# The two experts' weights by a tanh in the last stage of a graph and expert kernel

## The chip, the cores and the metric

The kernel runs on one core of a Trainium2 chip. The metric is the time of one execution on the device, in microseconds (us). A few runs of one kernel are given by their median.

## The reference

The input is x, 12,500 nodes of 256 features, with 212,500 weighted edges. A graph layer comes first (two rounds of a weighted sum over edges, with products by W1 and W2 and a batch norm between), and its result is added to x. Then comes a layer of 8 experts with the two best for each node:

```python
    x = x + _L0_gnn_ref(_layernorm(x, axis=-1), src, dst, edge_weight, L0_gnn_W1, L0_gnn_W2, L0_gnn_gamma, L0_gnn_beta)
    x = x + _L0_ffn_ref(_layernorm(x, axis=-1)[None], ...)[0]
...
            logits = tokens.astype(jnp.float32) @ router_w.astype(jnp.float32).T
            probs = jax.nn.softmax(logits, axis=-1)
            rw, re = jax.lax.top_k(probs, TOP_K)
            if TOP_K > 1:
                rw = rw / jnp.maximum(rw.sum(-1, keepdims=True), 1e-12)
            combine = jnp.zeros((N, E), tokens.dtype).at[jnp.arange(N)[:, None], re].set(rw)
            out = tokens
            for e in range(E):
                h = jax.nn.gelu(tokens @ w1[e] + b1[e], approximate=False)
                y = h @ w2[e] + b2[e]
                out = out + combine[:, e:e + 1] * y
```

With a and b the two largest logits of a node, the two weights are exp(a)/(exp(a)+exp(b)) and its complement to 1. That is 0.5 + 0.5 tanh((a-b)/2) and 0.5 - 0.5 tanh((a-b)/2).

## The kernel before

The program is written out by hand, engine by engine, with semaphores. The last stage (`pe_last`, `act_last`, `dve_last`, `pool_last`, `sp_last`) does three things at once. It gathers the rows of h2 for the second round of the graph layer, it makes the norm and the router's gates of a superblock, and it runs the 8 experts of the superblock before.

The nodes lie in 100 blocks of R = 125. SBS cuts them into 27 superblocks: 23 of 4 blocks and then 4 of 2 blocks. `moe_order` is called with the same order on every engine. In round t it takes three streams: the gather's chunks of superblock t, `first` (norm and router) of superblock t-1, and the experts of superblock t-2 (`up` is the first product with its Gelu, `down` the second product). After each expert's `up` it resumes `first` for one part, up to its next `yield`. Each `tick()` within them does one gather chunk.

A gather chunk is 128 gathered rows G (GpSimd, L1537). Two chunks of three are split: ScalarE writes the high half gH = G times weight (L1605), VectorE the low half gL (L1584), and TensorE multiplies both by a one-hot matrix (L1626, L1628). The third chunk stays whole (ScalarE L1601, TensorE L1624). VectorE makes the one-hot matrices, four chunks at once (L1571; L1567 for a block's tail). ScalarE and VectorE prepare a chunk LEAD = 5 chunks ahead of its product.

An expert's `up` is L1733 on TensorE, the Gelu at L1833 and the high half at L1838 on ScalarE, the low half at L1982 on VectorE; `down` is L1754 on TensorE and L1998 on VectorE, which adds the weighted result to Z. Both have two PSUM banks in turn.

The router is a part of `first`. TensorE multiplies by the router's weights (L1699) and signals d2_lg. VectorE takes the largest logit (L1929), subtracts it (L1931) and signals rt_s; then comes a tick. ScalarE waits for rt_s, takes Exp in place (L1812) and signals rt_e; it then does three ticks. VectorE waits for rt_e, sums (L1934), inverts (L1936) and multiplies (L1938). It then finds the eight largest in order, one MAX8 a block (L1941), and their positions, with one MATCH_VALUE_LOAD and one FIND_INDEX8 a block (L1944); a tick follows. Then it converts the positions (L1947), adds the two largest (L1948), bounds, inverts and multiplies (L1950, L1952, L1954), puts each of the two weights in its expert's place (L1958, L1959, one each a block), and adds the two (L1961), which signals rt_c; the third tick follows. TensorE waits for rt_c to turn the gates C (L1708), which ScalarE copies (L1820) for the product with b2 (L1714).

Earlier in `first` the norm takes its root on ScalarE (L1790, Sqrt), between VectorE's variance (L1895) and its reciprocal (L1898). ScalarE's loads of activation tables (ACT_TABLE_LOAD) are put in by the compiler and carry the line of the activation behind them. Every wait is on the waiting engine's own queue, in program order.

Of the kernel before, what the change touches and what calls it, by code (L numbers as in the profile page):

```python
# [9 lines left out]
ALU = mybir.AluOpType  # L10
ACT = mybir.ActivationFunctionType
AX = mybir.AxisListType
# [5 lines left out]
R = 125  # L18
# [137 lines left out]
def pairs_before(i):  # L156

    return sum(n // 2 for b, n in SBS[:i])


def l2_before(i, ex):

    return NEXP * pairs_before(i) + ex * (SBS[i][1] // 2)
# [31 lines left out]
def build(nc, x, src, dst, ew, W1, W2, gamma, beta, rw, w1, b1, w2, b2, out, force=None):  # L195
# [13 lines left out]
    with ExitStack() as ctx:  # L209
        def sb(name, shape, dt=F32):  # L210
            return ctx.enter_context(nc.sbuf_tensor(name, shape, dt))

        def sem(name):
            return ctx.enter_context(nc.semaphore(name))

        ident = sb("ident", [P, P])
        iota_f = sb("iota_f", [P, P])
# [189 lines left out]
        d2_tt, d2_tc, tsp, d2_lg, d2_k, rt_s, rt_e, rt_c = (sem(n) for n in ("d2_tt", "d2_tc", "tsp", "d2_lg", "d2_k", "rt_s", "rt_e", "rt_c"))  # L407
# [1101 lines left out]
        def bank(i, name, k=0):  # L1509

            z = SBS[i][1] // 2
            return psum[6 + ({"tr": 0, "z": 2, "tt": 2 + z, "lg": 4 + z, "ct": 5 + z, "b2": 6 + z}[name] + k) % 2]
# [249 lines left out]
        def act_last(e, B, gathered):  # L1762
            if gathered:
                for c in range(LEAD):
                    act_prepare(e, B, c)

            def chunks(t):
                b0, n = SBS[t]
                for o in range(b0 * KC, (b0 + n) * KC) if gathered else ():
                    if o + LEAD < NB * KC:  # L1770
                        act_prepare(e, B, o + LEAD)
                    yield

            def first(i, tick):
                b0, n = SBS[i]
                v, rt, TT = small[0:R, 570:598], B.rt, B.tT
                if i == 0:
                    e.wait_ge(wsp, 4 * WP)
                for k in range(2):
                    e.wait_ge(d2_tr, 2 * i + k + 1)  # L1780
                    if i and k == 0:
                        e.wait_ge(d2_z, pairs_before(i))
                    e.activation(B.zT[:, k * 512:k * 512 + n * R], bank(i, "tr", k)[:, 0:n * R], ACT.Copy).then_inc(d2_cp, 1)
                tick()
                yield
                for h in range(0, n, 2):
                    tick()
                yield
                e.wait_ge(d2_v, i + 1)
                e.activation(v[:, 12:12 + n], v[:, 8:8 + n], ACT.Sqrt).then_inc(d2_sq, 1)  # L1790
                tick()
                tick()
                yield
                for k in range(2):
                    e.wait_ge(d2_tt, 2 * i + k + 1)
                    if i and k == 0:
                        e.wait_ge(d2_lg, i)
                    if i >= 2 and k == 0:
                        e.wait_ge(l1s, 16 * (i - 1))
                    c_ = slice(k * 512, k * 512 + n * R)  # L1800
                    e.activation(TT[:, c_], bank(i, "tt", k)[:, 0:n * R], ACT.Copy).then_inc(d2_tc, 1)
                    e.activation(B.tH[i % 2][:, c_], bank(i, "tt", k)[:, 0:n * R], ACT.Copy).then_inc(d2_tc, 1)
                e.wait_ge(d2_k, 2 * (i + 1))
                for j in range(n):
                    c_ = slice(j * F, (j + 1) * F)
                    m = e.activation(B.Z(i)[:, c_], B.xt[:, c_], ACT.Identity, bias=v[:, 24 + j:25 + j], scale=v[:, 20 + j:21 + j])
                m.then_inc(d2_o, 1)
                tick()
                yield
                p8 = rt[:, 8:8 + 8 * n]  # L1810
                e.wait_ge(rt_s, i + 1)
                e.activation(p8, p8, ACT.Exp).then_inc(rt_e, 1)  # L1812
                tick()
                tick()
                tick()
                yield
                e.wait_ge(d2_ct, i + 1)
                if i:
                    e.wait_ge(d2_b2, pairs_before(i))
                e.activation(B.cT[:, 0:n * R], bank(i, "ct")[0:8, 0:n * R], ACT.Copy).then_inc(d2_cc, 1)  # L1820
                yield
                for h in range(0, n, 2):
                    tick()

            def up(i, ex, tick):
                n = SBS[i][1]
                for m_ in range(2):
                    q = 2 * (NEXP * i + ex) + m_
                    tick()
                    tick()  # L1830
                    f = psum[2 + q % 2][:, 0:n * R]
                    e.wait_ge(l1s, q + 1)
                    e.activation(f, f, ACT.Gelu, bias=b1T[:, ex, m_:m_ + 1]).then_inc(gel, 1)  # L1833
                    e.wait_ge(gel, q + 1)
                    if q >= 4:
                        o = NEXP * i + ex - 1
                        e.wait_ge(l2s, l2_before(o // NEXP, o % NEXP))
                    e.activation(B.hH[ex % 2][:, m_ * 512:m_ * 512 + n * R], f, ACT.Copy).then_inc(hhi, 1)  # L1838

            def down(i, ex, tick):  # L1840
                for j in range(SBS[i][1]):
                    tick()
            moe_order(chunks, first, up, down, nothing)

        def dve_last(e, B, own, gathered):
# [29 lines left out]
            def first(i, tick):  # L1875
                b0, n = SBS[i]
                Zs, X, C, rt = B.Z(i), B.xt, B.comb[i % 2], B.rt
# [41 lines left out]
                L = bank(i, "lg")[0:R, 0:8 * n].rearrange("p (b e) -> p b e", e=8)  # L1919

                def r(at, w=1):
                    return rt[:, at:at + n * w] if w == 1 else rt[:, at:at + n * w].rearrange("p (b e) -> p b e", e=w)

                def wide(a):
                    return a.rearrange("p (b o) -> p b o", o=1).broadcast_to([R, n, 8])
                p8, m8 = r(8, 8), r(48, 8)
                ix, ixf = rt[:, 88:88 + 8 * n].bitcast(U32), r(128, 8)
                e.wait_ge(d2_lg, i + 1)
                own.done(e.tensor_reduce(r(0), L, AX.X, ALU.max))  # L1929
                e.wait_ge(own.s, own.n)  # L1930
                e.tensor_tensor(p8, L, wide(r(0)), ALU.subtract).then_inc(rt_s, 1)  # L1931
                tick()
                e.wait_ge(rt_e, i + 1)
                own.done(e.tensor_reduce(r(0), p8, AX.X, ALU.add))  # L1934
                e.wait_ge(own.s, own.n)
                own.done(e.reciprocal(r(4), r(0)))  # L1936
                e.wait_ge(own.s, own.n)
                own.done(e.tensor_tensor(p8, p8, wide(r(4)), ALU.mult))  # L1938
                e.wait_ge(own.s, own.n)
                for j in range(n):  # L1940
                    own.done(e.max(m8[:, j, :], p8[:, j, :]))  # L1941
                e.wait_ge(own.s, own.n)
                for j in range(n):
                    own.done(e.max_index(ix[:, 8 * j:8 * j + 8], m8[:, j, :], p8[:, j, :]))  # L1944
                tick()
                e.wait_ge(own.s, own.n)
                own.done(e.tensor_copy(rt[:, 128:128 + 8 * n], ix))  # L1947
                own.done(e.tensor_tensor(r(0), m8[:, :, 0], m8[:, :, 1], ALU.add))  # L1948
                e.wait_ge(own.s, own.n)
                own.done(e.tensor_scalar(r(0), r(0), 1e-12, None, ALU.max))  # L1950
                e.wait_ge(own.s, own.n)
                own.done(e.reciprocal(r(4), r(0)))  # L1952
                e.wait_ge(own.s, own.n)
                own.done(e.tensor_tensor(m8, m8, wide(r(4)), ALU.mult))  # L1954
                e.wait_ge(own.s, own.n)
                g0, g1 = r(168, 8), r(208, 8)
                for j in range(n):
                    own.done(e.tensor_scalar(g0[:, j, :], iota_f[0:R, 0:8], ixf[:, j, 0:1], m8[:, j, 0:1], ALU.is_equal, ALU.mult))  # L1958
                    own.done(e.tensor_scalar(g1[:, j, :], iota_f[0:R, 0:8], ixf[:, j, 1:2], m8[:, j, 1:2], ALU.is_equal, ALU.mult))  # L1959
                e.wait_ge(own.s, own.n)  # L1960
                e.tensor_tensor(C[:, 0:8 * n].rearrange("p (b e) -> p b e", e=8), g0, g1, ALU.add).then_inc(rt_c, 1)  # L1961
                tick()
# [21 lines left out]
            def down(i, ex, tick):  # L1984
# [6 lines left out]
                for h in range(0, n, 2):  # L1991
# [4 lines left out]
                    for j in range(h, h + 2):  # L1996
                        a = Zs[:, j * F:(j + 1) * F]
                        e.scalar_tensor_tensor(a, psum[4 + q % 2][0:R, (j - h) * F:(j - h + 1) * F], C[:, 8 * j + ex:8 * j + ex + 1], a,  # L1998
                                               ALU.mult, ALU.add).then_inc(moe, 1)
            moe_order(chunks, first, up, down, nothing)  # L2000


# [503 lines left out]
```

## Time and profile before

| | |
|---|---|
| median of 3 runs | 4628.79 us (4623.98 to 4629.16) |
| the profiled execution | 4638.37 us, its span 4636.6 us |
| mean granted clock of TensorE over the span | 0.937 |
| busy over the span: TensorE | 3811.2 us, 82% |
| VectorE | 3319.8 us, 72% |
| ScalarE | 3034.7 us, 65% |
| GpSimd | 2864.8 us, 62% |
| router passes (L1929 to L1961) | 27, the first at 2159.55 us, the last at 4595.43 us |

The views name the engines PE (TensorE's products), PEld (its weight loads), DVE (VectorE), ACT (ScalarE), POOL (GpSimd) and SP (SyncE). A line such as L1929 is line 1929 of the kernel. The time in square brackets in a timeline is how long the engine stood idle before the row, with the instruction that ended the wait by the profile; "issue" and "remote" are waits for which it found none on the core. Tile names in the views are those of memory that is shared: "X" stands also for the router's tile rt and for Z.

### The profile page before, as it was taken

How to read it: one execution, taken by the hardware profiler on the slowest of the kernel's cores; microseconds unless marked ns; L12 is line 12 of the kernel's file. 1: busy time of each engine (PE TensorE's matmuls, PEld its weight loads, DVE VectorE, ACT ScalarE, POOL GpSimd, SP SyncE). 2: the span in 40 equal slices, each digit the busy share in tenths (PEclk: the TensorE clock that was granted, in tenths of full speed). 3: DMA queues.
4: the chain of work that ended last, by engine and by line, in shares of the span. 5: the costliest groups of instructions: out<-in, count | busy, mean ns of one | idle time of the engine just before them, and what ended most of it. 6: DMA issues, size and time to landing. Idle time of an engine off the chain costs nothing.

```text
span 4636.6 us, 84123 instructions
## 1 busy us (share of the span) xinstructions
PE 3811.2 (82%) x26914; PEld 3306.3 (71%) x26914; DVE 3319.8 (72%) x8731; ACT 3034.7 (65%) x6515; POOL 2864.8 (62%) x2961
## 2 busy tenths in 40 slices
PE   1688888888789999955788888888888888888988
PEld 1677877887677777744577777777777777777867
DVE  8788888888688888855466666666666666666655
ACT  3688888888777777753455555655556555555555
POOL 0377776777566666546766666666666666666541
PEclk9999999999899999975799999999999999989989
DMA  8788888887799898863333333333333333333221
GB/s 237 278 313 312 315 310 309 309 311 282 264 316 309 310 311 299 297 188 111 93 99 100 110 101 96 107 100 103 105 102 105 101 100 109 101 98 106 82 75 29
DMA packets 308793, 857.93 MB, mean 185 GB/s; under 512 B 47937, under 2 KB 133018, under 8 KB 305852
## 3 DMA queue, kind: packets, MB, share of 16 engines
q0 software_dynamic: 140032, 442.58, 29.1%
q1 hardware_dynamic: 166148, 396.53, 26.7%
q10 hardware_dynamic: 2172, 13.35, 0.8%
q8 instruction: 226, 3.70, 0.3%
q14 instruction: 215, 1.76, 0.1%
HBM read 545.71 MB, written 306.56 MB: 184 GB/s over the span
## 4 chain that ended last, share of the span: by engine, by line
PE 51%; DVE 15%; ACT 12%; issue 11%; another core or an unknown queue 6%; DMA 4%; POOL 2%; SPq 0%; ACTq 0%; DVEq 0%; POOLq 0%
PE ps L1733 10%; PE ps L1754 8%; PE ps L1624 4%; PE ps L1461 4%; PE ps L891 3%; DMA L<-msgd 3%; PE ps L849 2%; PE ps L1628 2%; PE ps L892 2%; PE ps L860 2%; PE ps L1626 2%; DVE S L1407 2%; PE ps L848 2%; ACT gH L1605 2%
## 5 line engine op out<-in xcount | busy, mean ns | idle before, releaser
L1537 POOL DMA_INDIRECT G<-h,tabT x1440 | 1481.6, 1029 | 809.5 <-issue 385.1
L956 ACT ACTIVATE A<-ps,A 128x256 f32<-128x256 f32 x1728 | 692.0, 514 | 94.0 <-PE ps L892 89.5
L1007 POOL DMA_INDIRECT msgd<-A,tabT x432 | 549.6, 1272 | 291.5 <-ACT A L956 196.5
L1833 ACT ACTIVATE ps<-ps,b1T 128x500 f32<-128x500 f32 (+1 forms) x432 | 267.7, 620 | 697.2 <-remote 381.4
L1605 ACT ACTIVATE gH<-G,tabT 128x256 fp32r<-128x256 f32 x960 | 454.4, 503 | 275.2 <-PE ps L1628 102.6
L1584 DVE SCALAR_TENSOR_TENSOR gL<-G,tabT,gH 128x256 fp32r<-128x256 f32 x960 | 448.9, 481 | 115.8 <-ACT gH L1605 59.8
L1998 DVE SCALAR_TENSOR_TENSOR X<-ps,X 125x256 f32<-125x256 f32 x800 | 347.4, 478 | 248.7 <-remote 200.6
L891 PE MATMUL ps<-winH,DT 128*128 128x256 f32 x1728 | 469.1, 304 | 63.5 <-issue 39.5
L1626 PE MATMUL ps<-gH,s 128*125 128x256 f32 x1067 | 353.0, 332 | 110.2 <-ACT gH L1605 60.1
L892 PE MATMUL ps<-winL,DT 128*128 128x256 f32 x1728 | 433.1, 283 | 0.0
L1628 PE MATMUL ps<-gL,s 128*125 128x256 f32 x1067 | 339.0, 319 | 73.9 <-DVE gL L1584 37.8
L891 PEld LDWEIGHTS ps<-winH,DT 128*128 128x128 f32 x1728 | 329.6, 191 | 80.4 <-issue 67.8
L1624 PE MATMUL ps<-G,s 128*125 128x256 f32 x960 | 329.4, 426 | 62.7 <-issue 32.4
L1626 PEld LDWEIGHTS ps<-gH,s 128*125 128x125 f32 x1067 | 217.8, 204 | 173.9 <-issue 143.1
L892 PEld LDWEIGHTS ps<-winL,DT 128*128 128x128 f32 x1728 | 331.4, 192 | 0.0
L1386 POOL TENSOR_TENSOR low<-L,mH 128x256 fp32r<-128x256 f32 x267 | 227.9, 854 | 163.3 <-issue 115.8
L946 ACT ACTIVATE DT<-ps,tabT 128x512 fp32r<-128x512 f32 x432 | 319.8, 741 | 6.3 <-DMA h<-A 4.1
L1628 PEld LDWEIGHTS ps<-gL,s 128*125 128x125 f32 x1067 | 216.9, 203 | 129.8 <-issue 57.6
L1407 DVE TENSOR_SCALAR S<-gap,L 128x125 fp32r<-128x125 f32 x1068 | 290.1, 335 | 26.8 <-DMA L<-msgd 26.7
L1388 POOL COPY tabT<-L 128x12 f32<-128x12 f32 x400 | 224.8, 576 | 131.0 <-DVE S L1407 68.4
L1352 ACT ACTIVATE mH<-L 128x1024 fp32r<-128x1024 f32 x267 | 269.2, 1046 | 49.0 <-DMA L<-msgd 48.9
L1571 DVE TENSOR_TENSOR s<-iota_f,tabT 128x500 fp32r<-128x500 f32 x400 | 268.9, 672 | 9.6 <-PE ps L1624 5.2
(338 smaller groups left out, 11076.3 us busy)
## 6 DMA issues: line engine op xcount, KB each, us to landing
L<-msgd SPq DMA_DIRECT2D x400, 520.0 KB, 5.7
A<-sbd SPq DMA_DIRECT2D x54, 861.0 KB
msgd<-A SPq DMA_DIRECT2D x100, 325.0 KB
G<-h,tabT POOLq DMA_INDIRECT x1440
winR<-h SPq DMA_DIRECT2D x108, 128.0 KB
A<-in_x SPq DMA_DIRECT2D x10, 1120.0 KB
h<-A ACTq DMA_DIRECT2D x10, 1120.0 KB
acc<-h SPq DMA_DIRECT2D x10, 1120.0 KB
```

What stands on the lines that cost most here:

```text
L891: e.matmul(o, d_, winH[g % 3][:, :], start=True, stop=False)
L892: m = e.matmul(o, d_, winL[g % 3][:, :], start=False, stop=True)
L956: e.activation(M[:, n, 0:F], psum[4 + v % 4][:, (n % 2) * F:(n % 2 + 1) * F], ACT.Identity, scale=M[:, n, F + 2:F + 3]).then_inc(evc, 1)
L1007: e.indirect_dma_start(msgd, bass.IndirectOffsetOnAxis(ap=idxI[g % 4][:, t:t + 1], axis=0), msg[g % 3][:, t * 4 * RW:(t + 1) * 4 * RW], No ...
L1407: m = e.tensor_scalar(S3[:, k, :].rearrange("p (a b) -> p a b", b=5), B.iota, L3[:, k, F + 1:F + 2], None, ALU.is_equal)
L1537: e.indirect_dma_start(B.G[c % GRL], None, of, bass.IndirectOffsetOnAxis(ap=tab3[:, m, 0:1].bitcast(I32), axis=0)).then_inc(gatl[c % GRL], 16)
L1584: e.scalar_tensor_tensor(B.gL[c % HR2][:, :], B.G[c % GRL], tab3[:, m, 2:3], B.gH[c % HR2][:, :].bitcast(F32), ALU.mult, ALU.subtract).the ...
L1605: e.activation(B.gH[c % HR2][:, :], B.G[c % GRL], ACT.Identity, scale=w_).then_inc(g_hi, 1)
L1624: m = e.matmul(psum[q][0:R, 0:F], Sc.bitcast(F32), B.G[c % GRL], start=k == 0, stop=False)
L1626: e.matmul(psum[q][0:R, 0:F], Sc, B.gH[c % HR2][:, :], start=k == 0, stop=False)
L1628: m = e.matmul(psum[q][0:R, 0:F], Sc, B.gL[c % HR2][:, :], start=False, stop=False)
L1733: m = e.matmul(psum[2 + q % 2][:, 0:n * R], wt[:, at:at + P], t[:, k * 512:k * 512 + n * R], start=s_ == 0, stop=s_ == 5)
```

## The change

ScalarE takes, in place of the Exp of all 8 logits, a Tanh of half the difference of the two largest. VectorE copies the logits, finds the eight largest and subtracts the second from the first, then signals rt_s; it looks up the positions and converts them while ScalarE works. After a tick it waits for rt_e and makes both weights by one multiply and add each. The softmax's sum, the two reciprocals, the two products, the second sum and its bound are gone. The number of ticks on each engine is the same; VectorE's first two now stand before and after the conversion of the positions.

```diff
-                p8 = rt[:, 8:8 + 8 * n]
                 e.wait_ge(rt_s, i + 1)
-                e.activation(p8, p8, ACT.Exp).then_inc(rt_e, 1)
+                e.activation(rt[:, 4:4 + n], rt[:, 0:n], ACT.Tanh, scale=0.5).then_inc(rt_e, 1)
...
                 e.wait_ge(d2_lg, i + 1)
-                own.done(e.tensor_reduce(r(0), L, AX.X, ALU.max))
-                e.wait_ge(own.s, own.n)
-                e.tensor_tensor(p8, L, wide(r(0)), ALU.subtract).then_inc(rt_s, 1)
-                tick()
-                e.wait_ge(rt_e, i + 1)
-                own.done(e.tensor_reduce(r(0), p8, AX.X, ALU.add))
-                e.wait_ge(own.s, own.n)
-                own.done(e.reciprocal(r(4), r(0)))
-                e.wait_ge(own.s, own.n)
-                own.done(e.tensor_tensor(p8, p8, wide(r(4)), ALU.mult))
+                own.done(e.tensor_copy(p8, L))
                 e.wait_ge(own.s, own.n)
                 for j in range(n):
                     own.done(e.max(m8[:, j, :], p8[:, j, :]))
                 e.wait_ge(own.s, own.n)
+                e.tensor_tensor(r(0), m8[:, :, 0], m8[:, :, 1], ALU.subtract).then_inc(rt_s, 1)
                 for j in range(n):
                     own.done(e.max_index(ix[:, 8 * j:8 * j + 8], m8[:, j, :], p8[:, j, :]))
                 tick()
                 e.wait_ge(own.s, own.n)
                 own.done(e.tensor_copy(rt[:, 128:128 + 8 * n], ix))
-                own.done(e.tensor_tensor(r(0), m8[:, :, 0], m8[:, :, 1], ALU.add))
-                e.wait_ge(own.s, own.n)
-                own.done(e.tensor_scalar(r(0), r(0), 1e-12, None, ALU.max))
-                e.wait_ge(own.s, own.n)
-                own.done(e.reciprocal(r(4), r(0)))
-                e.wait_ge(own.s, own.n)
-                own.done(e.tensor_tensor(m8, m8, wide(r(4)), ALU.mult))
+                tick()
+                e.wait_ge(rt_e, i + 1)
+                own.done(e.tensor_scalar(r(120), r(4), 0.5, 0.5, ALU.mult, ALU.add))
+                own.done(e.tensor_scalar(r(124), r(4), -0.5, 0.5, ALU.mult, ALU.add))
                 e.wait_ge(own.s, own.n)
                 g0, g1 = r(168, 8), r(208, 8)
                 for j in range(n):
-                    own.done(e.tensor_scalar(g0[:, j, :], iota_f[0:R, 0:8], ixf[:, j, 0:1], m8[:, j, 0:1], ALU.is_equal, ALU.mult))
-                    own.done(e.tensor_scalar(g1[:, j, :], iota_f[0:R, 0:8], ixf[:, j, 1:2], m8[:, j, 1:2], ALU.is_equal, ALU.mult))
+                    own.done(e.tensor_scalar(g0[:, j, :], iota_f[0:R, 0:8], ixf[:, j, 0:1], rt[:, 120 + j:121 + j], ALU.is_equal, ALU.mult))
+                    own.done(e.tensor_scalar(g1[:, j, :], iota_f[0:R, 0:8], ixf[:, j, 1:2], rt[:, 124 + j:125 + j], ALU.is_equal, ALU.mult))
                 e.wait_ge(own.s, own.n)
                 e.tensor_tensor(C[:, 0:8 * n].rearrange("p (b e) -> p b e", e=8), g0, g1, ALU.add).then_inc(rt_c, 1)
                 tick()
```

## Rows read from the trace of the kernel before

**Rows 1.** Windows, last stage: busy of PE, PEld, DVE, ACT, POOL; clock; DMA.

```profile
2300.00:4636.00 2336.00, 2017.31 (x11722) 1737.45 (x11722) 1527.78 (x4008) 1340.99 (x2720) 1461.90 (x1428) 0.93 0.34 97
```

**Rows 2.** Groups, from 2140 us: busy us, mean ns; idle before, releasers.

```profile
L1929 DVE TENSOR_REDUCE X<-ps 125x4 f32<-125x32 f32 x23 | 4.4, 190 | 22.4 <-remote 15.8 <-PE ps L1699 6.4
L1947 DVE CAST X<-X 125x32 f32<-125x32 uint32 x23 | 4.6, 199 | 0.3
L1948 DVE TENSOR_TENSOR X<-X 125x4 f32<-125x4 f32 x23 | 3.9, 171 | 0.0
L1950 DVE TENSOR_SCALAR X<-X 125x4 f32<-125x4 f32 x23 | 4.1, 178 | 5.0 <-DVE X L1948 3.9 <-issue 0.5
L1952 DVE RECIPROCAL X<-X 125x4 f32<-125x4 f32 x23 | 4.1, 178 | 6.5 <-DVE X L1950 6.0
L1954 DVE TENSOR_TENSOR X<-X 125x32 f32<-125x32 f32 x23 | 4.5, 195 | 5.2 <-DVE X L1952 4.7
L1812 ACT ACTIVATE X<-X 125x32 f32<-125x32 f32 x23 | 5.3, 231 | 23.5 <-issue 11.9 <-DVE X L1931 11.5
```

**Rows 3.** Who waited for L1961, and TensorE's group at L1628, from 2140 us.

```profile
  PE ps L1708: 17.3, 6
L1628 PE MATMUL ps<-gL,s 128*125 128x256 f32 x1023 | 318.6, 313 | 44.3 <-issue 29.9 <-DVE gL L1584 8.4 <-DVE X L1998 2.7
```

**Rows 4.** Timeline of one router pass: start us, us, engine, line, what.

```profile
2505.92 1.28 ACT L1812 ACT_TABLE_LOAD   x1
...
2508.10 0.19 DVE L1929 TENSOR_REDUCE X<-ps 125x4 f32<-125x32 f32 x1 [0.82 <-remote]
2508.32 0.19 DVE L1931 TENSOR_TENSOR X<-ps,X 125x32 f32<-125x32 f32 x1
...
2508.55 0.23 ACT L1812 ACTIVATE X<-X 125x32 f32<-125x32 f32 x1 [1.34 <-DVE X L1931]
...
2509.22 0.48 DVE L1584 SCALAR_TENSOR_TENSOR gL<-G,tabT,gH 128x256 fp32r<-128x256 f32 x1 [0.70 <-PE ps L1624]
...
2509.62 0.18 DVE L1934 TENSOR_REDUCE X<-X 125x4 f32<-125x32 f32 x1
...
2509.83 0.18 DVE L1936 RECIPROCAL X<-X 125x4 f32<-125x4 f32 x1
...
2510.04 0.19 DVE L1938 TENSOR_TENSOR X<-X 125x32 f32<-125x32 f32 x1
...
2510.27 0.37 DVE L1941 MAX8 X<-X 125x8 f32<-125x8 f32 x4
...
2515.49 0.19 DVE L1961 TENSOR_TENSOR X<-X 125x32 f32<-125x32 f32 x1 [0.63 <-DVE X L1959]
2515.60 0.51 DVE L1584 SCALAR_TENSOR_TENSOR gL<-G,tabT,gH 128x256 fp32r<-128x256 f32 x1
...
2516.16 0.45 PE L1628 MATMUL ps<-gL,s 128*125 128x256 f32 x1 [3.31 <-issue]
```

**Rows 5.** Window behind that stall, columns as in rows 1.

```profile
2516.30:2519.70 3.40, 3.40 (x11) 2.88 (x12) 2.60 (x8) 0.00 (x0) 2.48 (x4) 0.50 0.28 80
```

**Rows 6.** Timeline of another pass, around its Exp.

```profile
4079.22 0.23 ACT L1812 ACTIVATE X<-X 125x32 f32<-125x32 f32 x1 [3.00 <-issue]
4079.36 0.49 ACT L1601 ACTIVATE G<-G,tabT 128x256 f32<-128x256 f32 x1
...
4080.00 1.19 PE L1624 MATMUL ps<-G,s 128*125 128x256 f32 x2 [2.17 <-issue]
```

**Rows 7.** Groups of table loads, and timeline of one load for the Gelu.

```profile
L1833 ACT ACT_TABLE_LOAD x53 | 68.0, 1283 | 0.9
L1812 ACT ACT_TABLE_LOAD x27 | 34.6, 1283 | 0.5
...
3009.23 1.28 ACT L1833 ACT_TABLE_LOAD   x1
...
3010.53 0.65 ACT L1833 ACTIVATE ps<-ps,b1T 128x500 f32<-128x500 f32 x1
```

**Rows 8.** Timeline: TensorE and VectorE late at the same instant.

```profile
3007.12 0.62 PE L1733 MATMUL ps<-t2H,w1H 128*128 128x500 f32 x2 [1.08 <-issue]
3007.12 0.19 DVE L1954 TENSOR_TENSOR X<-X 125x32 f32<-125x32 f32 x1 [1.06 <-DVE X L1952]
```

More of the change, by code:

```diff
@@ L1922, in r @@
                     return rt[:, at:at + n * w] if w == 1 else rt[:, at:at + n * w].rearrange("p (b e) -> p b e", e=w)
-                def wide(a):
-                    return a.rearrange("p (b o) -> p b o", o=1).broadcast_to([R, n, 8])
                 p8, m8 = r(8, 8), r(48, 8)
```

## Prediction, made before the change was run

> **What bounds the kernel now.** The change touches the last stage only, so I read that stage first as a whole, then one pass of the edited code, then who waits for it. The busy times from 2300 us on give TensorE 2017 of 2336 us, VectorE 1528, ScalarE 1341, at a mean granted clock of 0.93 [rows 1]. TensorE is the bound, but not a full one: it stands still for about 320 us of this stage and runs part of the rest at the lower of its clocks. What VectorE or ScalarE save counts only where TensorE is standing still for it, and the question is how much of the 320 us that is.
>
> The timeline of one router pass answers it [rows 4]. VectorE takes the logits at 2508.10 and adds up the gate matrix C at 2515.49, 7.6 us later, nearly all in instructions of 0.16 to 0.3 us that wait for one another. In between it serves the gather's chunks only at two ticks; here one of them gave a gL. The next gL starts at 2515.60, right behind the last gate instruction, and TensorE's matmul of L1628, which reads a gL, starts at 2516.16, when that gL is done, after 3.31 us of standing still. The view says "issue" for this wait, but 0.05 us lie between the end of the gL (2516.11) and the matmul's start, and it is so at other such rows. So the router's serial chain on VectorE holds up the gather's low halves, and with them TensorE. In six passes (the first and the last five), the matmul that turns C (L1708) waits for L1961 itself: 17.3 us [rows 3].
>
> I then added up, over all 27 passes, TensorE's idle times of over 0.1 us between the start of L1929 and 1.5 us after the end of L1961: 73.7 us. In it are the 17.3 us at L1708, and 20.7 us at nine matmuls of L1628 that stand behind a gL queued after L1961 (3.31 us in [rows 4], 4.00 us the largest; the whole group at L1628 idles 44.3 us [rows 3]). The other 35.7 us: about 8 us at L1624, where ScalarE stood at its Exp and G came late [rows 6], and about 28 us of gaps labelled "issue", as at L1733 in 3007.12, where VectorE's next instruction came late at the same instant [rows 8].
>
> **VectorE, part by part**, for a superblock of 4 blocks. The removed steps by their distance from one start to the next: L1931 0.22 us (it goes with the largest-logit subtraction), L1934 0.21, L1936 0.21, L1938 0.23 [rows 4], the sum L1948 0.09 (it overlaps the cast), then L1950, L1952 and L1954 about 0.20, 0.20 and 0.22 by their durations of 178 to 195 ns plus the wait for their own semaphore [rows 2]: 1.58 us. L1929 is replaced by a copy of the same 32 elements, as long as the cast of L1947 (199 ns against 190) [rows 2, 4]: nothing. Added are one subtraction of 4 elements (0.15) and two tensor_scalars on 4 elements (0.30 with one wait): 0.45 us. The four MAX8, the eight index instructions, the cast and the nine gate instructions stay. Net 1.13 us.
>
> Two more things go. L1950, L1952 and L1954 have 16.7 us of idle before them over 23 passes, 0.73 us a pass [rows 2]; they are short waits on the instruction just before, beyond the usual 0.03 us, and some will only move to the instructions that stay. I take 0.5, between 0 and 0.73. And VectorE now waits for the Exp and the gH behind it: L1931 ends at 2508.51, its next work starts at 2509.22 [rows 4]. In the new order the eight index instructions (0.7 us) run while ScalarE does the tanh, but the tick's gL behind them still needs the gH that ScalarE makes after the tanh. I take 0.3 of 0.7. Together the pass becomes shorter by 1.9 us (1.1 to 2.6); for the four passes of 2 blocks, whose chain has none of those idle gaps, 1.4.
>
> What reaches TensorE: at L1708 two passes of 4 blocks and four of 2 give 2x1.9 + 4x1.4 = 9.4 us. At L1628 four stalls of over 3 us give 1.9 each, two of 1.95 and 1.98 the same, and three of 1.32, 1.20 and 0.54 all they have: 14.4 us. Of the 28 us of "issue" gaps I take 5 (0 to 20), since the trace doesn't tell what they wait for and the nearest row shows VectorE and TensorE late together.
>
> **The clock.** Behind the stall of 3.31 us the granted clock falls to 0.50, that is 1.2 instead of 2.4 GHz, from 2516.3 to 2519.7, with TensorE busy all through [rows 5]. Such a stretch of 3.4 us costs up to 1.7 us. A stall that is only shortened need not keep the clock up; I take five such stretches less: 8 us (0 to 20).
>
> **ScalarE.** The Exp gives way to a Tanh of 4 elements instead of 32 (231 ns now [rows 2]): nothing. The question is the tables. Now every pass has four loads: for Sqrt, back for Gelu, for Exp, back for Gelu; of 1283 ns each, 107 in all with the one of the first stage [rows 7]. If Tanh is served by the table that Gelu leaves loaded, 54 go, 70 us of ScalarE. Nearly all of it is covered. The load for the Exp is issued ahead of the wait for VectorE: at 2505.92, and the Exp still waits 1.34 us after it [rows 4]; where the Exp starts right after it, it is at most 0.45 us late. The load back is issued ahead of Gelu's wait for the up matmuls, and in 11 of 27 passes Gelu starts right behind it, as at 3010.53 [rows 7]; 11x1.3 = 14 us is the most that it can cost, and the hidden activations have two banks of slack. I take 3 us (0 to 14). If the load stays, this term is nothing.
>
> The rows show 1283 ns for a load and a Gelu that starts 0.02 us after it [rows 7]. The Trainium skill ("ScalarE: Activation LUTs", What ACT_TABLE_LOAD costs) gives a switch 1283 ns and a drain of about 1380 ns more, 2.66 us. By that 54 loads would be an estimated 144 us of ScalarE, the most for the 11 passes 29 us, and this term some 6 us in place of 3; no drain shows in these rows.
>
> One thing becomes worse. ScalarE stands at the tanh until VectorE has done the copy, four MAX8 and the subtraction: 0.22 + 0.41 + 0.15 us after the logits, with the wait about 0.85, against 0.45 now [rows 4]. Behind it on ScalarE are the gH and G of the next chunks. At 4079.22 the Exp came after 3.00 us of waiting, the G behind it was ready at 4079.85, and TensorE had stood 2.17 us for it at L1624 [rows 6]. In such passes the 0.4 us is paid in full, at most 27x0.45 = 12 us; five chunks are prepared ahead, so mostly it is not. I take 4 (0 to 12). Nothing changes on the DMA queues or on GpSimd.
>
> **Sum**: 9.4 + 14.4 + 5 + 8 + 3 - 4 = 36 us. The profiled execution took 4638.4 us (its span 4636.6), 9.6 over the median of the three, 4628.8; the stalls should be the same in both, so I take the 36 off the median: 4593 us, 0.8% less.
>
> **Rivals.**
> (a) The forecast, 4575 to 4610: chance 0.53.
> (b) Tanh is not in Gelu's table: the load for it and the load back stay, 107 in all, and the sum loses the 3 us: 4596, with 4580 to 4612. For it: the trace shows a load at each turn between Sqrt, Gelu and Exp and never at Copy or Identity (two of the three in [rows 7]); on Tanh it shows nothing. Chance 0.14. The Trainium skill (same page, Table sets: the hidden batching unit) speaks for this one: it lists tanh beside exp and beside sigmoid, and gelu in a set apart.
> (c) Handed on. TensorE's stall at L1628 moves to the next late operand (another gH, or the L1998 that are also queued behind the router), and only the 9.4 us at L1708 and a few us more come through: 4617 (4610 to 4625). For it: ScalarE and VectorE are both in program order, and TensorE also idles at L1626 and L1624 outside the router. Against it: VectorE has a third of the stage free [rows 1] and each stall read in the router ends with a gL. Chance 0.11.
> (d) More. Most of the 73.7 us and ten low stretches go: 60 to 75 us, 4560. Chance 0.13.
> (e) Nothing that can be measured: the gaps move to the instructions that stay: 4620 to 4638. Chance 0.05.
> (f) Slower: the longer stand of ScalarE at the tanh. It decides if the new chain's gain is off TensorE's path (its stalls being the G and gH behind that wait) and the 0.4 us a pass comes on it, with a low stretch of 1.7 us behind some: 27x0.45 + 5x1.7 = 21 us, 4650. Against it: only four passes show a stall at L1624 just behind the Exp. Chance 0.04.
>
> **Numbers.** Likeliest 4593. The range for 8 in 10 takes all of (a) to (c) but their edges and a part of (d): 4563 to 4622. A change under 0.2% (9 us) is about what a measurement of this kernel can't tell from none. Faster by more: (a), (b), (d) and most of (c), 0.87; within: 0.09; slower: 0.04.
>
> **What would show it.** The start of the copy to the end of the gate sum should take about 5.7 us where it was 7.6; the L1708 idle should fall from 17 to 8 us; the largest stalls at L1628 behind the router from over 3 to about 1.3 us; the table loads from 107 to 53 by (a), or 107 by (b); the mean granted clock should rise a little above 0.937. ScalarE's wait at the tanh should be longer than the 23.5 us at the Exp now [rows 2]. The prediction is wrong if the router pass is shorter by 2 us and TensorE's idle in it is what it was (c), or if the pass itself is not shorter (e).

## The result, and the profile after

| | before | after |
|---|---|---|
| median of 4 runs | 4628.98 us | 4598.42 us (4594.72 to 4602.53) |
| ratio | | 0.9936, 95% interval 0.9922 to 0.9951 |
| the profiled execution | 4638.37 us | 4594.72 us |
| table loads | 107 | 55 |
| router passes: mean from the start of the first step to the end of the last | 6.80 us | 4.50 us |

The change saves 30.6 us by the medians, where 36 were predicted (4593 us). The two profiled executions lie 43.9 us apart, since that of before lies 9 us above its kernel's median and that of after 4 us below its own; 8.9 of the 43.9 us arose ahead of the first router product, in code that is the same in both. The mean granted clock of the profiled execution is 0.936, where it was 0.937.

The router pass in the profile after, in the timeline (columns as in rows 4), at the place that answers to [rows 4]:

```profile
2497.61 0.19 DVE L1925 COPY X<-ps 125x32 f32<-125x32 f32 x1
...
2497.84 0.37 DVE L1928 MAX8 X<-X 125x8 f32<-125x8 f32 x4
...
2498.25 0.17 DVE L1930 TENSOR_TENSOR X<-X 125x4 f32<-125x4 f32 x1
...
2498.45 0.21 ACT L1811 ACTIVATE X<-X 125x4 f32<-125x4 f32 x1 [1.67 <-issue]
...
2499.09 0.48 DVE L1584 SCALAR_TENSOR_TENSOR gL<-G,tabT,gH 128x256 fp32r<-128x256 f32 x1
...
2501.68 0.19 DVE L1946 TENSOR_TENSOR X<-X 125x32 f32<-125x32 f32 x1
2501.79 0.48 DVE L1584 SCALAR_TENSOR_TENSOR gL<-G,tabT,gH 128x256 fp32r<-128x256 f32 x1
...
2503.35 0.28 PE L1628 MATMUL ps<-gL,s 128*125 128x256 f32 x1
```

From the copy to the end of the gate sum it is 4.26 us where it was 7.58. VectorE no longer stands for the gH behind the Exp, as the index instructions fill the time. The next gL is ready at 2502.27, a microsecond before TensorE reads it at 2503.35, and the stall of 3.31 us is gone. The same holds over all passes: added up as in the prediction (idle times of over 0.1 us from the first VectorE instruction of a router pass to 1.5 us after its last), TensorE's idle time is 25.6 us where it was 73.7, and the largest stall at L1628 in it is 1.15 us where it was 4.00. A part of this fall is only that the passes, and so the stretches looked at, are shorter.

The groups of table loads and of the tanh, which answer to [rows 2, 7]:

```profile
L1832 ACT ACT_TABLE_LOAD x27 | 34.6, 1283 | 0.5
...
L1811 ACT ACTIVATE X<-X 125x4 f32<-125x4 f32 x23 | 4.7, 205 | 48.8 <-DVE X L1930 36.2 <-issue 12.6
...
L1811 ACT ACT_TABLE_LOAD x1 | 1.3, 1283 | 0.0
```

Only the very first Tanh has a load of its own; from then on Tanh is served by what Gelu has loaded. ScalarE's idle time before this step doubled, from 23.5 to 48.8 us. That comes from the loads and not from the later start of the Tanh: it is 52.5 us in e1, with the old chain and without the load that used to fill a part of the wait, and 24.3 in e2, with the new chain and the load.

TensorE's groups after, over the last stage, against [rows 3] (idle before them is the number behind the second bar):

```profile
L1708 PE MATMUL ps<-ident,X 125*8 125x125 f32 x100 | 16.3, 284 | 4.2 <-DVE X L1946 4.2
L1628 PE MATMUL ps<-gL,s 128*125 128x256 f32 x1024 | 316.4, 310 | 22.7 <-issue 14.4 <-DVE gL L1584 5.0
...
L1733 PE MATMUL ps<-t1H,w1L 128*128 128x500 f32 (+1 forms) x448 | 184.2, 426 | 16.9 <-issue 16.6
L1733 PE MATMUL ps<-t1H,w1H 128*128 128x500 f32 (+1 forms) x448 | 154.4, 425 | 37.2 <-DVE h1L L1967 23.1 <-issue 13.8 <-ACT gH L1605 0.2
L1754 PE MATMUL ps<-w2H,h2L 128*125 128x256 f32 x800 | 169.6, 290 | 21.1 <-issue 20.8
```

Three of these groups in the profile of before, which were not shown there:

```profile
L1733 PE MATMUL ps<-t1H,w1L 128*128 128x500 f32 (+1 forms) x448 | 190.6, 440 | 4.9 <-issue 4.6
L1733 PE MATMUL ps<-t1H,w1H 128*128 128x500 f32 (+1 forms) x448 | 160.5, 438 | 25.7 <-DVE h1L L1982 14.5 <-issue 10.6 <-ACT gH L1605 0.4
L1754 PE MATMUL ps<-w2H,h2L 128*125 128x256 f32 x800 | 165.9, 286 | 8.3 <-issue 7.7
```

Summed over all TensorE groups of a line, the idle time before them went down by 13.1 us at L1708 (17.3 to 4.2), 21.6 at L1628 (44.3 to 22.7), 19.8 at L1624 (63.8 to 44.0) and 5.9 at L1626 (94.3 to 88.4). It went up by 22.2 us at L1733 (74.2 to 96.4) and 13.3 at L1754 (49.8 to 63.1), the experts' products. So 60 us were taken off TensorE's waits and 35 of them came back at other instructions. These are two single executions, so the same sums are set beside those of two pairs of the experiments below (us, new chain less old; e9 and e10 are both kernels on one chip, e1 is the kernel before without its loads and e5 the changed one, on two chips):

| pair | L1708 | L1628 | L1624 | L1626 | L1733 | L1754 |
|---|---|---|---|---|---|---|
| before, after | -13.1 | -21.6 | -19.8 | -5.9 | +22.2 | +13.3 |
| e1, e5 | -5.3 | -18.6 | -0.1 | -4.8 | +17.6 | -0.3 |
| e9, e10 | -9.2 | -22.7 | +2.9 | -1.5 | +9.0 | +0.2 |

What all three show is the gain at L1708 and L1628 and the loss at L1733. The changes at L1624 and L1754 are those of the first pair alone.

### The profile page after: what moved, and what is told of

Read it like the earlier page. It is cut to its first block, busy times and chain, and to the rows that moved or that the text cites. A ratio compares the mean times of both kernels' runs of the same rounds, so it can differ in the third digit from the quotient of the medians.

```text
span 4592.6 us, 83936 instructions
## 1 busy us (share of the span) xinstructions
PE 3802.9 (83%) x26914; PEld 3311.6 (72%) x26914; DVE 3296.9 (72%) x8596; ACT 2959.0 (64%) x6463; POOL 2838.2 (62%) x2961
## 3 DMA queue, kind: packets, MB, share of 16 engines
q0 software_dynamic: 140032, 442.58, 29.5%
## 4 chain that ended last, share of the span: by engine, by line
PE 51%; DVE 16%; ACT 11%; issue 11%; another core or an unknown queue 5%; DMA 3%; POOL 2%; SPq 0%; ACTq 0%; DVEq 0%; POOLq 0%
PE ps L1733 10%; PE ps L1754 8%; PE ps L1624 4%; PE ps L1461 3%; PE ps L891 3%; DVE S L1407 3%; PE ps L892 2%; PE ps L849 2%; PE ps L1628 2%; PE ps L860 2%; PE ps L1626 2%; DVE low L1411 2%; PE ps L848 2%; ACT A L956 2%
## 5 line engine op out<-in xcount | busy, mean ns | idle before, releaser
L1537 POOL DMA_INDIRECT G<-h,tabT x1440 | 1465.8, 1018 | 790.9 <-issue 374.1
L1626 PE MATMUL ps<-gH,s 128*125 128x256 f32 x1067 | 352.1, 331 | 101.2 <-ACT gH L1605 57.9
L1628 PE MATMUL ps<-gL,s 128*125 128x256 f32 x1067 | 336.4, 316 | 53.0 <-issue 25.0
L1624 PE MATMUL ps<-G,s 128*125 128x256 f32 x960 | 326.2, 422 | 47.7 <-issue 25.9
L1626 PEld LDWEIGHTS ps<-gH,s 128*125 128x125 f32 x1067 | 217.9, 204 | 165.7 <-issue 132.1
L1352 ACT ACTIVATE mH<-L 128x1024 fp32r<-128x1024 f32 x267 | 268.8, 1045 | 44.3 <-DMA L<-msgd 43.3
L1628 PEld LDWEIGHTS ps<-gL,s 128*125 128x125 f32 x1067 | 217.1, 204 | 99.6 <-DVE gL L1584 39.6
L1411 DVE TENSOR_TENSOR low<-L,mH 128x768 fp32r<-128x768 f32 x267 | 264.9, 992 | 11.3 <-ACT mH L1352 11.3
```

The source lines that it names most:

```text
L1537: e.indirect_dma_start(B.G[c % GRL], None, of, bass.IndirectOffsetOnAxis(ap=tab3[:, m, 0:1].bitcast(I32), axis=0)).then_inc(gatl[c % GRL], 16)
L1624: m = e.matmul(psum[q][0:R, 0:F], Sc.bitcast(F32), B.G[c % GRL], start=k == 0, stop=False)
L1626: e.matmul(psum[q][0:R, 0:F], Sc, B.gH[c % HR2][:, :], start=k == 0, stop=False)
L1628: m = e.matmul(psum[q][0:R, 0:F], Sc, B.gL[c % HR2][:, :], start=False, stop=False)
```

## Where in the stage the time arose

TensorE runs the same 26,914 matmuls in the same order in all kernels here, so the start of one and the same matmul can be compared. I split the stage at the first router product (L1699) of the 1st, 2nd and 23rd pass. Times in us, worked out from those starts and the end of the span; 21 passes lie between the 2nd and the 23rd.

| kernel | 1st to 2nd | 2nd to 23rd | 23rd to the end | together |
|---|---|---|---|---|
| before | 159.3 | 2048.8 | 272.4 | 2480.6 |
| after | 153.0 | 2033.4 | 259.1 | 2445.6 |
| difference | -6.3 | -15.4 | -13.3 | -35.0 |

More than half of it comes from the edges. From the 23rd pass on TensorE waits for the gates themselves: the idle time at L1708 there falls from 12.2 to 0.5 us, which is 11.7 of the 13.3 us. Between the first two passes it falls by only 1.4 of the 6.3 us, and the rest lies at other lines. A middle pass saves 0.7 us, though its router pass is over 2 us shorter. The experiments ask whether the chain is the cause at all, and where the rest goes.

## The experiments

Theory A: TensorE waits for VectorE's serial router chain, and the gain is its shortening. Theory B: the gain is the table loads that ScalarE no longer does. The experiments ran on three chips, and the kernel before takes 4657 us (e1 to e4), 4655 us (e5 to e8) and 4272 us (e9 to e12) on them; which chip the first measurement was made on is not on record. Single runs of a kernel scatter by 5 to 10 us there, so each ratio is to be read with its interval. The ratio and the quotient of the medians can differ: for e5 the ratio gives 10 us and the medians 15.6.

### e1: the tables alone

```diff
-                e.activation(p8, p8, ACT.Exp).then_inc(rt_e, 1)
+                e.activation(p8, p8, ACT.Tanh).then_inc(rt_e, 1)
```

> The kernel before with Tanh written in place of Exp at L1812 and nothing else; the gates are then not the reference's. All steps of VectorE stay, the table loads should fall from 107 to 54. Theory A (VectorE's serial router chain is what TensorE waits for): about -3 us, between 0 and -8, that is 4621 to 4629 where the kernel before takes 4629. Theory B (the 54 loads on ScalarE are the gain): -15 us or more.

Measured: 4652.12 us, 0.9990 (0.9972 to 1.0007). The loads fell to 55, VectorE's chain stayed at a mean of 6.83 us. The group of loads for Gelu:

```profile
L1833 ACT ACT_TABLE_LOAD x27 | 34.6, 1283 | 0.5
```

So 52 loads of 1.28 us were taken away and at most 13 us followed, with 5 us by the medians. Theory B, in its form of 15 us or more, falls; the prediction's term of 3 us (0 to 14) stands, but the interval also holds nothing.

### e2: the new chain with all the loads

```diff
-                e.activation(rt[:, 4:4 + n], rt[:, 0:n], ACT.Tanh, scale=0.5).then_inc(rt_e, 1)
+                e.activation(rt[:, 4:4 + n], rt[:, 0:n], ACT.Exp, scale=0.5).then_inc(rt_e, 1)
```

> The changed kernel with Exp in place of Tanh, all else as changed; the two weights are then wrong. 107 table loads again. Theory A: within 5 us of the changed kernel, some 4598 to 4604, so -25 to -31 against the kernel before. Theory B: 4613 or more, less than half of the gain left. If e1 and e2 disagree, the loads count only once the chain is short.

Measured: 4636.30 us, 0.9956 (0.9939 to 0.9973), with 107 loads. The chain alone gives 21 us (13 to 28), a little under the 25 to 31 expected and well over what theory B leaves. Together with e1 this is theory A: the loads lie beside other work.

### e3 and e4: the edges alone, the middle alone

Each engine takes the new steps under a condition and the old ones otherwise (e3; e4 has `0 < i < NS - 5` in its place):

```diff
+                if i == 0 or i >= NS - 5:
...
+                else:
...
```

> The change in six router passes alone (the first and the last five), the old chain in the 21 passes between. By the times at which the same matmuls start in the two profiles, the stage gained 35 us, of which 6 between the first and second router pass and 15 from the 23rd pass on. Theory A with the gain at the edges: -18 to -23 us, 4606 to 4611. By the prediction's own terms (9.4 us at L1708 and a part of the clock): -12 us, 4617.

> The change in the 21 passes in the middle alone, the old chain in the first and the last five. By the profiles 14 us in 21 passes: 4613 to 4617. If the middle passes hand their gain on entirely (rival c) it is within 5 us of the kernel before, above 4624; by the prediction's terms (14.4 + 5 + 8 + 3 - 4 = 26 us) it is 4603. e3 and e4 together should make up the whole -31 us if the passes are independent.

Measured: e3 0.9954 (0.9936 to 0.9972), 20 us; e4 0.9991 (0.9975 to 1.0008), 7 us. The six passes at the edges give three quarters of the 27 us that the two have together. The 21 passes in the middle, with four fifths of the shortened chain, give 0 to 12 us. The prediction's terms had it the other way round, 12 at the edges and 26 in the middle (a part of the clock's 8 us is in both).

### e5: the changed kernel again

> The changed kernel once more, beside the next three on one chip. It gave 0.9936 of the kernel before; e3 (edges alone, 0.9954) and e4 (middle alone, 0.9991) together give 0.9945. If the passes add up it stays between 0.993 and 0.996. Its profile beside the first one also shows how far two profiles of one kernel differ in the place where a time arises.

Measured: 4639.18 us, 0.9979 (0.9963 to 0.9994); by the medians 15.6 us. That is outside the 0.993 to 0.996 expected. Its router pass takes 5.03 us in the mean where the first profile had 4.50. The interval doesn't meet that of the first measurement (0.9922 to 0.9951), which was taken from four runs a side.

### e6 and e7: a shorter chain still

e6 makes the 8 gate instructions as 2 over both experts and all blocks. e7 finds the gates by comparing the logits with the two largest values, and needs neither positions nor their conversion; two equal largest logits would give other weights.

The edit of e7:

```diff
-                for j in range(n):
-                    own.done(e.max_index(ix[:, 8 * j:8 * j + 8], m8[:, j, :], p8[:, j, :]))
...
+                own.done(e.tensor_tensor(gg, pp, mm, ALU.is_equal))
                 tick()
-                e.wait_ge(own.s, own.n)
-                own.done(e.tensor_copy(rt[:, 128:128 + 8 * n], ix))
...
+                own.done(e.tensor_tensor(gg, gg, ww, ALU.mult))
```

> The changed kernel with the 8 gate instructions of a pass (4 in a small one) made as 2 over all blocks and both experts at once: VectorE's router pass about 1.1 us shorter (0.3 in the four small ones), ScalarE untouched. Theory A with all of it on TensorE's path: 2x1.1 + 4x0.3 + 21x1.1 = 27 us less than e5. Theory A' (full at the edges, a fifth in the middle, as e3 and e4 suggest): 3.5 + 5 = 8 us less. Rival c (handed on in the middle): 3 us less.

> The changed kernel with the gates found by comparing the logits with the two largest values, without positions: the 8 index instructions and the cast go too, some 2.1 us less VectorE time a pass than e5, 1.0 in the small ones. Two equal largest logits of one node would give other weights. Theory A': 2x2.1 + 4x1.0 = 8 us at the edges and a fifth of 44 = 9 in the middle, 17 us less than e5. Rival c: 8 us less. All on the path: 50 us less.

Measured: e6 4629.22 us, 0.9950 (0.9932 to 0.9968), by the medians 10 us less than e5; e7 4624.81 us, 0.9941 (0.9921 to 0.9961), 14 us less than e5. The mean router passes are 3.20 and 2.73 us long, so e6 took 1.8 us off a pass and not 1.1. Both came out near the weak form (8 and 17 us), though the interval of e6 meets that of e5: on this chip each microsecond taken off the chain in all 27 passes is worth some 7 us at the end, 4 to 9 by the interval ((1 - 0.9941) x 4655 us over 6.8 - 2.7 us, with e1's 6.83 us for the old chain), about a quarter of the 27 us of chain.

### e8: ScalarE's tick ahead of its wait

```diff
+                tick()
                 e.wait_ge(rt_s, i + 1)
                 e.activation(rt[:, 4:4 + n], rt[:, 0:n], ACT.Tanh, scale=0.5).then_inc(rt_e, 1)
-                tick()
                 tick()
                 tick()
```

> The changed kernel with ScalarE's first gather tick moved ahead of its wait for the tanh. It measures the term that the prediction put at +4 us (0 to 12): ScalarE standing at the tanh while chunks wait. If it is real, e8 is 3 to 8 us below e5 and TensorE's waits at L1624 and L1626 for ScalarE shrink just behind the router; if it is not, e8 is within 2 us of e5.

Measured: 4638.94 us, 0.9968 (0.9953 to 0.9984). It is 0.2 us from e5 by the medians and 5 us by the ratios, and the intervals overlap widely, so the times alone can't tell 4 us from none. The trace shows nothing of it either: TensorE's idle time at L1624 and L1626, which was to shrink, is 59.8 and 85.5 us where e5 has 57.9 and 83.1. If ScalarE's stand at the tanh has a price, it is too small to be found here.

### e9 and e10: both kernels on a faster chip

> The kernel before against itself, for two things: how far the ratio of a kernel to itself lies from 1 on this chip (within 0.998 to 1.002 by theory), and a profile of it beside those of e1 to e8, which ran on chips where it takes some 4655 us instead of 4629. The router pass should again take 6.5 to 7 us from L1929 to the end of L1961.

> The changed kernel a third time, beside e9, since 0.9936 and 0.9979 (e5) hardly agree. If the gain is a property of the kernel and e5 had bad luck, 0.994 to 0.996; if the gain depends on the chip, it is near 0.997 where the kernel before takes 4655 and near 0.994 where it takes 4629.

Measured: e9 1.0003 (0.9992 to 1.0014), so the comparison is sound. e10 4255.43 us, 0.9962 (0.9947 to 0.9976), 17 us. This chip is 8% faster, and the middle of the stage alone took 1785 us instead of 2049. The changed kernel has 0.9962 where the kernel before takes 4272 us, 0.9936 where it takes 4629 and 0.9979 where it takes 4655, so the gain doesn't go one way with the speed of the chip. The intervals of e5 and e10 overlap, and whether the gain depends on the chip stays open. The two profiled executions lie 41.8 us apart where the medians lie 17 apart; 12.9 of them arose ahead of the first router product and 28.8 in the stage, so the splits by place below are larger than the mean gain.

The profile of e9 names what ends TensorE's waits at L1628, where [rows 3] said "issue" for most of them. TensorE's groups of the last stage in e9, then the same two in e10:

```profile
L1628 PE MATMUL ps<-gL,s 128*125 128x256 f32 x1020 | 310.0, 305 | 43.6 <-DVE gL L1584 40.2
L1708 PE MATMUL ps<-ident,X 125*8 125x125 f32 x100 | 15.7, 277 | 13.7 <-DVE X L1961 13.7
```

```profile
L1628 PE MATMUL ps<-gL,s 128*125 128x256 f32 x1020 | 311.5, 307 | 20.9 <-DVE gL L1584 16.8
L1708 PE MATMUL ps<-ident,X 125*8 125x125 f32 x100 | 15.5, 274 | 4.5 <-DVE X L1946 4.5
```

With the same matmuls laid side by side, the middle passes show where the time goes. Between the 20th and the 80th matmul behind the router's first product, e10 needs 2.06 us less than e9 (11.36 against 13.42 us, means of 21 passes), as the shorter chain should give. Between the 140th and the 220th, some 26 to 39 us later, it needs 1.48 us more (14.08 against 12.60). What is left is 0.5 us a pass. What holds it is told by GpSimd's gathers in e9 and by ScalarE's wait for them (groups from 2300 to 4200 us):

```profile
L1537 POOL DMA_INDIRECT G<-h,tabT x1254 | 1285.4, 1025 | 402.0 <-issue 296.8 <-DVE gL L1584 43.0 <-PE ps L1624 38.7
```

```profile
L1605 ACT ACTIVATE gH<-G,tabT 128x256 fp32r<-128x256 f32 x838 | 407.6, 504 | 278.5 <-DMA G<-h,tabT 271.0 <-PE ps L1628 2.3 <-PE ps L1624 2.3
```

From the 2nd to the 23rd pass a gather takes 1.025 us in the mean, and the gap before it has a median of 0.305 us; in e9 to e12 no gap there is over 0.4 us. A pass has 64 gathers, 64 x (1.025 + 0.305) = 85.1 us, and a middle pass takes 85.0 us. ScalarE waits 271 us for gathers to land. So GpSimd sets the length of the middle passes on this chip, one gather right behind the other. A TensorE that is early at the router finds the later chunks not yet there.

On the first chip that is not so: a middle pass takes 97.6 us, GpSimd waits there for TensorE to free a buffer (95.9 and 85.0 us of its group's idle time, for L1624 and L1628; 175 of its 1344 gaps in the middle passes are over 0.4 us), and yet only 0.7 us a pass is left. In the profiles of before and after, the 20th to the 80th matmul give 1.58 us (14.09 to 12.51) and the 80th to the 140th take back 0.97 (11.42 to 12.39). In the latter the time at the lower clock rises from 0.18 to 1.14 us a pass, and the gaps at L1754 from 0.2 to 0.7. For the pair e1 and e5, old and new chain (on two chips on which the kernel before takes 4657 and 4655 us), it is much the same: 0.99 us given and 1.49 taken back, the time at the lower clock there from 0.13 to 1.03 us; the 0.97 us that e5 is shorter between the 140th and the 220th matmul make up its gain of 0.5 us a pass.

### e11: the chain filled up again

```diff
+                for _ in range(12 if True else 0):
+                    own.done(e.tensor_copy(rt[:, 252:252 + n], rt[:, 0:n]))
+                    e.wait_ge(own.s, own.n)
                 own.done(e.tensor_scalar(r(120), r(4), 0.5, 0.5, ALU.mult, ALU.add))
```

> The changed kernel with 12 more copies of 4 elements, one waiting for the other, ahead of the two weights: some 2.4 us more VectorE chain in each pass, which makes the router pass as long as that of the kernel before, with the 54 table loads still gone. Theory A: all of the gain is lost, 0.998 to 1.001 of the kernel before. Theory B (loads) or a gain from the earlier tanh: it keeps most of it, 0.996 or less.

Measured: 4284.46 us, 1.0026 (1.0014 to 1.0038). All of the gain is gone and some more, with 55 loads. The filling was too long: the mean router pass is 7.13 us against 5.99 in e9. One place of it, in the timeline:

```profile
2519.90 0.19 DVE L1949 TENSOR_TENSOR X<-X 125x32 f32<-125x32 f32 x1
2520.01 0.48 DVE L1584 SCALAR_TENSOR_TENSOR gL<-G,tabT,gH 128x256 fp32r<-128x256 f32 x1
...
2520.54 0.58 PE L1628 MATMUL ps<-gL,s 128*125 128x256 f32 x1 [3.94 <-DVE gL L1584]
```

This is the stall of [rows 4] made again by nothing but VectorE instructions, and the view now names the gL. It can be counted in every trace, since the gL and the matmuls of L1628 pair off in order (1067 of each). The stalls of matmuls that start within 0.12 us of the end of their gL, where that gL began within 1.5 us of the end of a router pass, add up to 31.4 us in e9, 8.6 in e10 and 49.5 in e11, at 14 matmuls each; to 16.9 us before and 0.7 after; to 11.6 in e1, with the old chain and the loads gone, and 0.6 in e2, with the new chain and the loads kept. This is the plainest evidence for theory A, and it settles what the "issue" of [rows 4] was.

### e12: the shortest chain and the early tick

> e7 (gates by comparing with the two largest values) and e8 (ScalarE's first tick ahead of the tanh) together. e7 gave 0.9941 and e8 0.9968 where the changed kernel gave 0.9979. If both add: 0.993; if the tick does nothing: 0.994.

Measured: 4247.28 us, 0.9944 (0.9928 to 0.9960), 8 us less than e10 by the medians, with intervals that overlap. By the ratio it is nearer to what was expected if the tick does nothing, but the interval holds the 0.993 as well. The mean router pass is 2.33 us. By the place in the stage (us, as in the table above):

| kernel | router pass, mean | 1st to 2nd | 2nd to 23rd | 23rd to the end |
|---|---|---|---|---|
| e11, chain refilled | 7.13 | 134.8 | 1787.1 | 243.1 |
| e9, before | 5.99 | 134.7 | 1785.4 | 234.7 |
| e10, changed | 4.22 | 128.1 | 1774.9 | 223.1 |
| e12, mask and tick | 2.33 | 130.0 | 1769.5 | 221.1 |

Over nearly 5 us of difference in the chain, the 21 middle passes move by 18 us, 0.8 us each. With GpSimd at its limit such a pass can become shorter only by its gathers, and the sums agree: over the 21 passes the gathers themselves take 1376 us in e9, 1365 in e10, 1378 in e11 and 1360 in e12, and the gaps between them 409 or 410 in all four. The last five move by 22 us, 4.4 us each, with router passes of 5.7 us in e11 and 1.9 in e12 (their means over the five): there the chain counts in full.

## Why the prediction was right, and where its terms were off

The forecast (a) was 4593 us within 4563 to 4622, and 4598.4 was measured. Its direction held in every run with the chain shortened in all passes, and its mechanism (TensorE waits for the gL queued behind the router, and at the edges for the gates) is seen in the traces and made again in e11; the loads behave as (a) said, and (b) is out with 55 of them. The sign named for (c), that TensorE's idle time in the router passes stays, did not show: it fell from 73.7 to 25.6 us, and from 68.9 in e9 to 29.5 in e10. The mean clock, which was to rise a little, did not.

That the number is so near is in part luck. On the other three chips the time saved was 16 to 21 us by the medians (10 to 20 by the ratios) for the changed kernel or its chain alone (e5, e10, e2), about half of the 36 us, so the 30.6 us of the first measurement is the upper end of what was seen.

- The router pass: 1.9 us shorter predicted, 2.3 measured (6.80 to 4.50); 1.8 in e9 and e10. The short idle times before L1950, L1952 and L1954 were taken at 0.5 us; in e9, with the old chain, they are only 0.8 to 0.9 us over 23 passes for each, where [rows 2] has 5.0 to 6.5.
- L1708: 9.4 us predicted, 13.1 measured (9.2 in e9 and e10). The whole edge was under-sized, 13.3 us from the 23rd pass on, nearly all at L1708, and 6.3 between the first two, where L1708 is 1.4 of them and the rest was not taken apart.
- L1628: 14.4 us predicted, 21.6 measured (22.7 in e9 and e10).
- "Issue" gaps: 5 us of gain predicted. They did not go: at L1733 and L1754 together TensorE's idle time rose by 35.5 us (17.3 from e1 to e5, 9.2 from e9 to e10). This is the step that was missing. Rival (c), the gain handed on, is right for most of the gain in the middle passes and wrong for the edges; I had priced (a) as if nothing came back.
- The clock: 8 us predicted. The time at the lower clock in the stage went from 407 to 400 us, which at half the speed is 3.5 us at most. The lower clock behind the router became less (from 3.74 to 2.01 us a pass between the 20th and 80th matmul), but it became more right behind that (from 0.18 to 1.14).
- The table loads: 3 us predicted, 5 us by e1's medians with an interval that holds nothing and 13. 52 of them went, not 54, as the first Tanh still has one, and so has the Gelu behind it.
- ScalarE's longer stand: 4 us lost predicted. The later start came as worked out (0.83 us behind VectorE's first instruction in the mean of 23 passes, 0.48 before), but it isn't what made the 48.8 us, as e1 and e2 show, so that sign came true for another reason. Its price was not found: L1624, where it should have shown, idles 19.8 us less in the first pair and 2.9 us more in e10 than in e9, and e8 finds nothing.

So the sum was near through errors that offset each other: in the first pair the waits at L1624, L1628 and L1708 gave twice what was put down for them, and the experts' products took 35 us back. The Trainium skill ("ScalarE: Activation LUTs", Table sets: the hidden batching unit) lists tanh with exp and with sigmoid and not with gelu. Here Tanh is served by the set that Gelu has loaded: 55 loads, one of them at a Tanh. Of the drain of about 1380 ns that the Trainium skill adds to a load (same page, What ACT_TABLE_LOAD costs), no row here shows anything: the Gelu of [rows 7] starts 0.02 us after its load.

What is open: what the gaps named "issue" at L1733 and L1754 wait for, and why those at L1733 grew. In e6 and e7 the idle time at L1733 is 68.6 and 63.8 us, no more than e1's 68.2, though the chain is shorter still. On the chip of e9 such gaps are nearly absent, and a middle pass is 12.6 us shorter there; no experiment told what differs between the chips.

## What to carry to other kernels

Look for what is queued behind a serial chain of tiny instructions on an engine in program order: the chain's price was not paid by its own result (the gates) in most passes but by the next operand queued behind it (gL). Price the passes at the edges of a pipeline apart from those in its middle: a microsecond off the chain was worth one or somewhat more at the last five passes and a sixth to a third of one in the middle (e11 against e12; before against after), where on one chip the next limit, GpSimd's gathers, stood close behind, and on the others a part came back as time at the lower clock and as gaps of unknown cause. A table load that stands ahead of a wait costs its engine 1.28 us and may cost the kernel little: 52 of them, 67 us of ScalarE, were worth 5 us here, with an interval from nothing to 13.

## What the runs showed of the hardware

- One and the same kernel took 4657, 4655 and 4272 us on three chips, and 4629 us in the first measurement, whose chip is not on record. In the last stage of e9 TensorE's idle time is 5.9 us a middle pass where it is 12.7 in the profile of before, and its time at the lower clock falls from 407 to 194 us.
- On the chip of e9 to e12 the mean duration of a gather (L1537, in the middle passes) goes with the length of VectorE's router pass: 1024.5 ns in e9 and 1024.6 in e11, but 1014.3 in e10 and 1012.6 in e12. With 64 gathers a pass the 10 ns are 0.65 us, about what a middle pass of e10 saves. The gathers that run beside the router pass itself are not the long ones (970 ns in e9, 974 in e10). What the gathers take over their median of 957 ns differs most from 8 to 16 us after the router pass began, when VectorE works off what queued behind it: 0.98 us a pass in e9 and 0.91 in e11, but 0.34 in e10 and 0.07 in e12. In the first 8 us it is the other way round, 0.19 and 0.12 against 0.45 and 0.41. On the other chips it is less clear: 1024 ns before and 1015 after, but 1018 in e1 with the old chain and 1018 in e2 with the new one. No run took apart what makes these gathers longer.
